# Two attentions of an image tower on one core: samples in a pipeline, products from split operands, scores taken twice

## What is computed

```python
# 1. an attention-free token mixer; x is (32, 64, 256, 4), so 256 tokens of 256 features a sample
q, k, v = proj(Wq, bq), proj(Wk, bk), proj(Wv, bv)
ew = exp(w_bias * local_mask)                     # 256 x 256
y = sigmoid(q) * (ew @ (exp(k) * v)) / (ew @ exp(k))
h = layernorm(y @ out_w + out_b + flatten(x))
h = concatenate([cls_tok, h])                     # 257 tokens
# 2. cosine attention, 16 heads, q and k of 16, v of 64 features a head
t = layernorm(h)
q, k, v = l2norm(t @ Wq), l2norm(t @ Wk), l2norm(t @ Wv)
out = square(relu(q @ k.T)) @ v
h = h + (tanh(norm(out)) * out / norm(out)) @ Wout
# 3. latent attention, 16 heads of 16, causal, and a mixture of experts
t = layernorm(h); r = rmsnorm(t)
q = r @ Wq; c = r @ Wdkv; k = c @ Wuk; v = c @ Wuv
t = t + softmax(causal(q @ k.T / 4)) @ v @ Wo
h = h + t + moe(rmsnorm(t))                       # 2 of 8 experts a token
```

## Time and profile before

| | |
|---|---|
| median of 3 executions | 6577.85 us (6570.84 to 6599.03) |
| the profiled execution | 6628.06 us |
| its span | 6626.3 us |
| the mixer loop, from the first to the last L670 | 3200.4 us |
| the latent loop, from the first to the last L1274 | 1922.3 us |
| after it | 1137 us |

### The profile page before, as it was taken

The page is one execution under the profiler, slowest core; times in us unless marked ns, Lnnn a source line. Parts: engine busy times, 40 slices in busy tenths (PEclk is TensorE's granted clock), DMA queues, the critical chain, the costliest instruction groups (busy, mean ns, idle before and its releaser), DMA issues. The chain is left out here.

```text
span 6626.3 us, 76195 instructions
## 1 busy us (share of the span) xinstructions
PE 5112.9 (77%) x23484; PEld 3241.9 (49%) x23485; DVE 2896.4 (44%) x7551; ACT 1832.3 (28%) x5049; POOL 729.4 (11%) x630
## 2 busy tenths in 40 slices
PE   5788888888888888888847888988988982214994
PEld 3454454544545445454524555555555552213994
DVE  3444444444444444444414454454454443222443
ACT  1222222222222222222213333333333332101442
POOL 1000000000000000000050000000000001223442
PEclk7766767667676676766756776676676665556997
DMA  1000000000000000000000000000000003122447
GB/s 39 9 9 5 9 5 9 9 5 9 5 9 9 5 9 5 9 9 5 6 2 17 15 10 15 13 11 15 12 12 15 10 13 101 54 99 56 76 76 195
DMA packets 139491, 165.38 MB, mean 25 GB/s; under 512 B 15378, under 2 KB 120083, under 8 KB 139460
## 3 DMA queue, kind: packets, MB, share of 16 engines
q1 hardware_dynamic: 104964, 121.36, 6.0%
q0 software_dynamic: 25968, 35.15, 3.2%
q10 hardware_dynamic: 8528, 8.52, 0.4%
HBM read 84.04 MB, written 80.93 MB: 25 GB/s over the span
## 5 line engine op out<-in xcount | busy, mean ns | idle before, releaser
L614 DVE TENSOR_TENSOR PR<-psA,R 128x516 f32<-128x516 f32 x512 | 352.4, 694 | 635.4 <-ACT R L486 634.4
L1155 ACT ACTIVATE m_P<-psC,m_nmax 128x129 f32<-128x129 f32 (+1 forms) x1024 | 420.6, 418 | 653.4 <-DVE m_nmax L1239 650.3
L764 PE MATMUL psA<-PR,V 128*64 128x258 f32 x2048 | 568.8, 662 | 1.0
L486 ACT ACTIVATE R<-psA 128x516 f32<-128x516 f32 x512 | 304.4, 600 | 736.8 <-PE psA L754 733.3
L1232 DVE COPY m_PT<-psC 128x256 f32<-128x256 f32 (+1 forms) x512 | 284.8, 556 | 410.1 <-PE psC L1347 409.6
L1347 PE MATMUL psC<-ident,m_P 128*128 128x128 f32 x1536 | 419.6, 405 | 56.8 <-ACT m_P L1155 56.8
L1359 PE MATMUL psC<-m_PT,m_V 128*16 128x128 f32 x3072 | 374.6, 371 | 11.8 <-DVE m_PT L1232 11.8
L799 PE MATMUL psA<-wout,OT 128*128 128x256 f32 x1024 | 362.3, 531 | 0.0
L1347 PEld LDWEIGHTS psC<-ident,m_P 128*128 128x128 f32 x1536 | 234.9, 196 | 235.8 <-issue 125.1
L1659 PE MATMUL psR<-identd,d_tn 128*128 128x128 f32 x130 | 31.1, 426 | 396.4 <-DVE d_tn L1586 396.4
L1239 DVE TENSOR_REDUCE m_nmax<-psC 128x2 f32<-128x258 f32 (+1 forms) x512 | 285.3, 557 | 105.6 <-PE psC L1335 98.3
(11 more groups left out here) (371 smaller groups left out, 9270.5 us busy)
## 6 DMA issues: line engine op xcount, KB each, us to landing
e_x<-xg SPq DMA_DIRECT2D x143, 129.0 KB
xraw<-in_x SPq DMA_DIRECT2D x64, 256.0 KB, 3.8
odd_rows<-zeros SPq DMA_DIRECT2D x66, 128.0 KB
d_x<-xs SPq DMA_DIRECT2D x13, 640.0 KB
f_even<-out_rows SPq DMA_DIRECT2D x13, 640.0 KB
f_odd<-odd_rows SPq DMA_DIRECT2D x13, 640.0 KB
out_rows<-f_even ACTq DMA_DIRECT2D x13, 640.0 KB, 5.6
hs<-h SPq DMA_DIRECT2D x32, 256.0 KB, 2.0
```

The costliest lines, as they stand in the source:

```text
L486: act.activation(R[:, h % 2], ps[:, b:b + 2, 0:QCOLS], ACT.Relu).then_inc(relu_done, 1)
L614: dve.tensor_tensor(PR[:, h % 3], ps[:, b:b + 2, 0:QCOLS], R[:, h % 2], ALU.mult).then_inc(prob_done, 1)
L764: last = pe.matmul(ps[64 * hh:64 * hh + 64, 4 + pr % 2, 0:QCOLS], V[:, t, h * DV:(h + 1) * DV], PR[:, u % 3, hh, :], start=False, stop=Tru ...
L1155: act.activation(PM[:, u % 2, hh, 0:N - 1], ps[:, b + hh, 0:N - 1], ACT.Exp, bias=nmax[:, t, h:h + 1], accum_out=esum[:, t, h:h + 1]).then ...
```

## The change

The routing and expert stages stay. The rest is rewritten in four places.

- `mixer_and_attention`: a helper `samples` runs the first sample, a loop over two samples at a time, and the last. In a sample's body, the eight head pairs of sample i stand in each queue with the front of sample i+1 and the scaling and output projection of sample i-1 between them; what both need has two buffers. Queries and keys are projected turned, in fp32, and aren't scaled: four heads lie in 128 rows, 32 apart (`parity` zeroes half of each copy of the keys), and a score product has 32 rows. The keys' inverse squared lengths go into the values (`value_rows` on POOL, with a power over 16 columns and a product over 1024), the queries' into the output scale. `inverse_root` goes; the output's roots are one POOL power over 32 columns (`output_roots`). The values are products of split operands, `xh`, `xl` (tokens) with `wvh`, `wvl` (weights), three fp32r products for one fp32. All scores of a pair are made before its relu; R is 1024 wide, and DVE squares it from SBUF. Class scores come from class weights `wkc` and `wqc` (80 columns for three parts). PE sums the squares of queries and keys (`norm_sums`). POOL keeps a copy of h1.
- `class_tokens`: the lengths are computed as [128, 2, 2], 4 values a row instead of 256, spread and turned afterwards.
- `latent_attention`: pipelined over the samples in the same manner, by four groups of four heads. Scores are taken query by key for the maxima (`scores`, `maxima`), the maxima are turned and join the queries as a further row (`turn_maxima`, `lower_queries`), and the scores are taken again, key by query (`lowered_scores`), so that ACT's exponential gives the turned probabilities. `weigh` writes four heads side by side with a column of ones for the sum; `turn_back` and `divide` finish. The padded weights `wukp`, `wqp` put heads 32 apart.
- `load_constants`: `wv` and `wout` come in reordered pieces (8 transfers each), the split weights and padded weights are built on DVE, the class token's products go through a row in HBM and some 25 small DVE operations, POOL builds a mask on 80 rows and the class values `vcls3`. The padded output weights `wo_pad` go.

The diff, cut to its core:

```diff
-def inverse_root(dve, y, x, work, stepped, before):
...
+            dve.tensor_copy(v.wvh[:], v.wv[:]).then_inc(wv_high, 1)
+            dve.wait_ge(wv_high, 1)
+            dve.tensor_tensor(v.wvl[:], v.wv[:], v.wvh[:].bitcast(F32), ALU.subtract)
...
+        def samples(eng, body, last_body):
+            body(0, 0, False, True)
+            with eng.Fori(0, (nb - 2) // 2) as n:
+                body(2 * n + 1, 1, True, True)
+                body(2 * n + 2, 0, True, True)
+            body(nb - 1, (nb - 1) % 2, True, False)
+            last_body(nb - 1, (nb - 1) % 2)
...
+            def value_rows(j, e, t):
+                pool.wait_ge(v_lift, 2 * j + t + 1)
+                power(pool, vrn[:, t], vsm[:, t], v.inv_root).then_inc(v_rn, 1)
+                pool.wait_ge(v_rn, 2 * j + t + 1)
+                pool.wait_ge(k_inv, j + 1)
+                pool.tensor_tensor(vc[:, t], vrn[:, t], rk[:, t], ALU.mult).then_inc(v_c, 1)
+                pool.wait_ge(v_c, 2 * j + t + 1)
+                pool.tensor_tensor(V[:, e, t].rearrange("p (g d) -> p g d", d=DV),
+                                   Vr[:, t].rearrange("p (g d) -> p g d", d=DV),
+                                   vc[:, t].unsqueeze(2).to_broadcast([P, HEADS, DV]), ALU.mult).then_inc(v_ready, 1)
...
+            def output_roots(i):
+                pool.wait_ge(o_lift, i + 1)
+                power(pool, orr[:], osm[:], v.inv_root).then_inc(o_rooted, 1)
...
+            def sample(i, d, before, more):
+                if before:
+                    output_roots(i - 1)
+                if more:
+                    norm_roots(i + 1)
+                keep_h1(i, d)
+                if more:
+                    class_parts(i + 1, 1 - d)
+                    value_rows(i + 1, 1 - d, 0)
+                    value_rows(i + 1, 1 - d, 1)
...
+            def relu(i, p):
+                act.wait_ge(sim_done, PAIRS * i + p + 1)
+                need(act, prob_done, PAIRS * i + p - 1)
+                act.activation(R[:, p % 2], ps[:, 0:2, :].rearrange("p a (t n) -> p a t n", t=LT),
+                               ACT.Relu).then_inc(relu_done, 1)
...
+            def prob(i, d, p):
+                dve.wait_ge(relu_done, PAIRS * i + p + 1)
+                need(dve, av_done, PAIRS * i + p - 1)
+                dve.wait_ge(acl_done, i + 1)
+                dve.tensor_copy(PR[:, p % 2, :, :, L],
+                                acl[:, d, :, 2 * p:2 * p + 2].rearrange("p t h -> p h t"))
+                dve.tensor_tensor(PR[:, p % 2, :, :, 0:L], R[:, p % 2], R[:, p % 2], ALU.mult).then_inc(prob_done, 1)
...
+                cols = slice(half * 512, (half + 1) * 512)
+                for k in range(KT):
+                    pe.matmul(ps[:, bank, :], xh[:, k, t * P:(t + 1) * P], v.wvh[:, k, cols], start=k == 0, stop=False)
+                    pe.matmul(ps[:, bank, :], xh[:, k, t * P:(t + 1) * P], v.wvl[:, k, cols], start=False, stop=False)
+                if n == 0:
+                    pe.wait_ge(xl_done, j + 1)
+                for k in range(KT):
+                    last = pe.matmul(ps[:, bank, :], xl[:, k, t * P:(t + 1) * P], v.wvh[:, k, cols], start=False,
+                                     stop=k == KT - 1)
+                last.then_inc(v_done, 1)
...
+            def sim(i, d, p):
+                c, m, g = p // 4, p // 2 % 2, p % 2
+                if p == 0:
+                    pe.wait_ge(qT_copied, i + 1)
+                    pe.wait_ge(kT_copied, 2 * i + 2)
+                need(pe, relu_done, PAIRS * i + p)
+                for t in range(LT):
                     for hh in range(2):
+                        rows = slice(32 * (2 * g + hh), 32 * (2 * g + hh) + 32)
+                        last = pe.matmul(ps[:, hh, t * L:(t + 1) * L], kT[rows, d, m, c, t * P:(t + 1) * P],
+                                         qT[rows, d, c, :], start=True, stop=True, skip_group_check=True)
+                last.then_inc(sim_done, 1)
...
+            def attend(i, d, p):
+                if p == 0:
+                    pe.wait_ge(p_ready, i + 1)
+                    pe.wait_ge(v_ready, 2 * i + 2)
+                need(pe, ss_done, PAIRS * i + p - 1)
+                pe.wait_ge(prob_done, PAIRS * i + p + 1)
+                pe.matmul(ps[:, 2 + p % 2, 0:QCOLS], v.vcls3[:, p * P:(p + 1) * P], v.pcl[:, d, :], start=True,
+                          stop=False, skip_group_check=True)
+                for t in range(LT):
                     for hh in range(2):
+                        n = 2 * p + hh
+                        last = pe.matmul(ps[64 * hh:64 * hh + 64, 2 + p % 2, 0:QCOLS], V[:, d, t, n * DV:(n + 1) * DV],
+                                         PR[:, p % 2, hh, t, :], start=False, stop=True, skip_group_check=True)
+                last.then_inc(av_done, 1)
...
+            def sample(i, d, before, more):
+                j = i + 1
+                sim(i, d, 0)
+                if more:
+                    mixer_inputs(j)
+                if before:
+                    square_sums(i - 1, 7)
+                sim(i, d, 1)
+                attend(i, d, 0)
+                if more:
+                    mix_keys(j)
+                sim(i, d, 2)
+                if more:
+                    mix_values(j)
+                attend(i, d, 1)
+                square_sums(i, 0)
+                if more:
+                    residual(j)
+                if before:
+                    turn_scale(i - 1, more)
+                sim(i, d, 3)
+                if before:
+                    spread_scale(i - 1, 0, more)
+                    spread_scale(i - 1, 1, more)
...
-        nrm = sbuf(nc, ctx, "b_nrm", [P, NP])
+        nrm = sbuf(nc, ctx, "b_nrm", [P, NT, 2])
...
+                for t in (1, 0):
+                    cols, keys_t = (slice(0, SEQ), SEQ) if t else (slice(SEQ, SEQ + 1 + P), 1 + P)
+                    for h in range(4):
+                        rows = slice(32 * h, 32 * h + 32)
+                        last = pe.matmul(ps[:, h, cols], qT[rows, d, g, t * P:(t + 1) * P], kT[rows, d, g, 0:keys_t],
+                                         start=False, stop=True, skip_group_check=True)
+                last.then_inc(s_done, 1)
...
+            def lowered_scores(i, d, g):
+                pe.wait_ge(qx_done, 4 * i + g + 1)
+                for t in range(LT):
+                    for h in range(4):
+                        rows = slice(32 * h, 32 * h + 32)
+                        last = pe.matmul(ps[:, h, t * L:t * L + (2 - t) * P], kT[rows, d, g, 1 + t * P:1 + (t + 1) * P],
+                                         qx[rows, g % 2, t * P:L], start=False, stop=True, skip_group_check=True)
+                        if t and h % 2:
+                            last.then_inc(t_done, 1)
+                pe.matmul(ps[0:4, OB + g % 2, L:2 * L], kb[:, d, g, :], qx[:, g % 2], start=True, stop=True,
+                          skip_group_check=True).then_inc(c_done, 1)
...
+                for t in range(LT):
+                    for h in range(4):
+                        pe.matmul(ps[32 * h:32 * h + 32, OB + g % 2, t * P:L], V[:, d, t, 4 * g + h, :],
+                                  PT[:, g % 2, h, t * L:t * L + (2 - t) * P], start=t == 0, stop=False,
+                                  skip_group_check=True)
+                pe.matmul(ps[:, OB + g % 2, 0:L], vc[:, d, g, :], pcT[:, g % 2, :], start=False, stop=True,
+                          skip_group_check=True).then_inc(pv_done, 1)
...
+            def maxima(i, g):
+                dve.wait_ge(s_done, 4 * i + g + 1)
+                for t in range(LT):
+                    cols = slice(0, SEQ) if t else slice(SEQ, SEQ + 1 + P)
+                    dve.tensor_reduce(nm[:, t, :, DK], ps[:, 0:4, cols], AX.X, ALU.max,
                                       negate=True).then_inc(max_done, 1)
+            def lower_queries(i, d, g):
+                dve.wait_ge(nm_done, 4 * i + g + 1)
+                dve.tensor_tensor(qx[:, g % 2], ps[:, OB + g % 2, L:2 * L], qT[:, d, g], ALU.add).then_inc(qx_done, 1)
...
+                scores(i, d, 0)
+                if before:
+                    weigh(i - 1, 1 - d, 3)
+                if behind:
+                    turn(j)
+                turn_maxima(i, 0)
+                mask_keys(i, 0)
+                lowered_scores(i, d, 0)
+                if before:
+                    turn_back(i - 1, 2, True)
+                if behind:
+                    latent(j)
+                if before:
+                    turn_back(i - 1, 3, True)
+                scores(i, d, 1)
+                weigh(i, d, 0)
+                if before:
+                    turn_output(i - 1)
```

More of the change, by code:

```diff
@@ L672, in _, with mixer_inputs @@
+            samples(dve, sample, last)
         @block.tensor
         def _(pe):
-            with pe.Fori(0, nb) as i:
-                pe.wait_ge(x2_ready, i + 1)
+            def mixer_inputs(j):
+                pe.wait_ge(x2_ready, j + 1)
```

(36 more changed lines are left out.)

1864 lines of the change are left out of this document (1086 added, 778 removed).

## The result

The changed kernel takes 4360.5 us (median of four executions, 4358.6 to 7739.6) beside 6574.5 us of the kernel before: a ratio of 0.6626, with a 95% interval of 0.6606 to 0.6647. One of the four took 7739.6 us; the comparison leaves it out, and its cause stays open. The profiled execution took 4361.4 us.

What follows compares the result with a forecast made beforehand. PE bounds the kernel, at half clock in the heads, alternating with chains of small steps in the fronts. Samples of 70 and 35 us plus fronts, ends and other stages sum to 4670, times 0.992 gives 4630 us; range 4300 to 5150.

Steps and rivals of the forecast that it cites:

- the forecast's own case: Whole program: the forecast of 4400 to 4950 us, given a chance of 0.60.
- rival 1: Both loops: full clock and no SBUF lock, samples of 58 and 33 us, 4215 us, to 4400 with part lock; chance 0.12.
- waits, 4: First loop: walking all four engines' written order at full clock gave 57.8 us a sample, 4 of it PE waits.
- clock, 6.5: First loop: an eighth of the work at 1.2 GHz adds 6.5 us a sample; ends 0 and 48.
- the three turns named: First loop, PE waits: first score after the last relu, values after the token split, scale turn; 4 us together.
- (a): First loop: POOL's powers lock SBUF against DVE's R x R, adding 5.7 us a sample; ends 0 and 10.
- the 2 for the chain: Second loop: PE's 31 us beside a chain of 30 to 34 us for four groups was taken as 33.
- the 2 for the clock: Second loop: 2 us a sample added for clock and start-up, giving 35 instead of 62.0.
- Hops in place of the waits (2): Both loops: score-bank rounds and locks replace waits, a third at 1.2 GHz; 84 and 43 us, 5290 total; chance 0.18.
- single 32-row tiles (4): Scores in both loops: 32-row tiles don't run side by side, +7 and +22 us a sample, 5500 total; chance 0.04.
- The clock at 1.2 GHz in both loops (3): Both loops: overlap won but clock lost, 107 and 62 us a sample, 6540 total; chance 0.06.
- what would show it: Signs in the new profile: addition distances, clock, first R x R beside the power, 41-us rows gone, PE over 80% busy.

## Why the prediction was right, and where its terms were off

The prediction was 4630 us in a range of 4300 to 5150. Its sign and the frame of its mechanism are what happened: PE's work bounds both loops, and the clock is mostly up. But the time lies 6% below, and 40 us below the 4400 at which the forecast's own case began; 4360 is in the band of rival 1 (4215 to 4400), half of which the range took in. That it lies inside the range is owed in part to that margin. Against the forecast's sum of 4670, the span of 4360 is 310 less:

- **Mixer, 207 less** (79.6 to 2139.8, 2060 instead of 43 + 2100 + 54 + 50 + 20 = 2267). A steady sample took 63.1 us instead of 70, which is all of it. PE's work, 54, measured 55.2; waits, 4, measured 3.3; clock, 6.5, measured 4.5. The size of the waits was lucky: of the three turns named, only the scale turn holds PE up (0.9 us); the others are the first square (1.5), the output's scaling (0.5) and the input copy (0.4). The term that failed is (a), "the first square can stand behind the 5.5-us power", 5.7 with the value rows: 0. PE does wait 1.5 us for that square, but since the small copy stands ahead of it in DVE's queue, not for the power. The power's price was right (5.42 us for 32 columns, 2.90 for 16), its hold on SBUF was not: the earlier trace rows shows a product, and I took it as the nearest row for a power. The runs with the plain product and with two powers show both sides: a product blocks, a power doesn't, and the power's real danger is its result, with 3.5 us to spare. The 2.5 us that I gave the value rows' product of 1024 columns are 1.90 in the trace.
- **Latent, 97 less** (1044 instead of 1141). A steady sample took 31.9 us instead of 35. PE's work, 31, was nearly right (31.5); the 2 for the chain and the 2 for the clock fell away. The chain's long part lies beside the weighing, and the clock stays at 1.00. Of the chain only the hop from the turn to the lowered scores is tight.
- **Class stage**: 45 instead of 47. **Start**: the first input product at 79.6, beside 77 for the start of the sample. **The rest**: 1131 instead of 1138.

The rivals: full clock and no lock (1) is half of what happened; no lock, but full clock in the second loop alone, where the first loses 4.5 us a sample. Hops in place of the waits (2) and single 32-row tiles (4) are out: PE's wait for a relu is 0.6 us in all, and eight records of the scores take 1.07 us, sixteen on four tiles in the second loop 0.94. The clock at 1.2 GHz in both loops (3) isn't in any of the rows; but the run without the overlap shows where it lives. The heads' products without a front among them run at 0.50 with PE busy 21.50 of 21.50 us.

Of "what would show it", the clock above 0.85, the power of 5 to 6 us, the two 41-us rows gone (now 1.01 each) and PE over 80% busy came true. The distances of 70 and 35 us didn't (63.1 and 31.9), nor did the late or long first square beside the power.

## What to carry to other kernels

Interleaving independent samples pays twice on TensorE: its waits are filled (half of 42.8 us here), and the clock is kept up (the other half), most likely by the wide products that then stand among the narrow ones, while the cheaper products by themselves brought nothing in the first loop. After such a change, read each remaining wait of PE in one steady sample and ask what stands in front of its producer in the producer's own queue: moving a few short steps took another 5% with no work removed. Before a step is moved, its result's spare time must be taken at the clock that the change will bring, not at the one in the trace.

## What the runs showed of the hardware

- POOL's power took 5.42 us on 32 columns of 128 rows while DVE multiplied in SBUF beside it at full speed (1.22 us); started inside such a product it took 6.34 us. A product of POOL over 1024 columns (1.89 us) held up a DVE copy of four columns until it ended.
- With PE busy all the time, narrow and short products ran at 0.50 (21.5 us in one sample), and the same kinds of products interleaved with wide ones at 1.00 over 37.5 us, PE busy for 36.4. Six more wide products a sample raised the mean clock from 0.94 to 0.96.
- A delay of PE cost more than its length where it let the clock fall: a square that started 1.6 us late made the sample 3.3 us longer, 1.5 of it in PE's wait, with the clock at 0.89 instead of 0.92.
